# Output stage: the order of loads behind stores, one-hots made on two engines, and a shorter lag of the last step

## The chip, the core and the metric

The kernel runs on one core of a Trainium2 chip. A core has TensorE (PE), VectorE (DVE), ScalarE (ACT), GpSimd (POOL) and SyncE (SP, which here only issues DMAs). Each works through its own instruction stream in order, and they wait for each other by semaphores. The metric is the device time of the program in microseconds (us).

## What is computed

A layer of an xLSTM kind of attention with a decay (the first stage), then a layer in which a router lets each of 16 experts pick 2 of the 32 positions along the first axis, for each of the 512 places of the second, attend among the picked, and add their outputs back, followed by a residual and a layer norm. The part that matters here is the end:

```python
ao = jnp.einsum('hbid,hde->hbie', av, Wo) + bo
outs = jnp.zeros_like(t).at[b_ids, tok].add(ao)
y = t + outs
yn = (y - mu) * jax.lax.rsqrt(var + 1e-05) * ln_g + ln_b
# and, outside the layer: x = x + yn, x of shape (32, 512, 512), float32
```

Adding the experts' rows back to their tokens is a matrix product with a one-hot matrix: `hot[i, j] = (tokid[j] == colv[i])`.

## The kernel before

The program has three stages on one core: `recurrence_stage` (the largest part of the span), `expert_stage`, and `output_stage`, from 1398 us on. Only the last is touched. It works in **tiles** T = 0 to 127 of 128 rows by 512 elements; four tiles are a **half** H = 0 to 31 (1 MB), which is what SP loads and stores, in four DMAs each way. Five buffers `xt` (`x1_half0` to `x1_half3` and a part of `v_all`) hold the halves in turn.

The order of work is written out by hand, per engine:

- **SP** loads the first five halves (`load`, L1304). Then, for each half H, it waits until the half's four tiles are finished, stores it (L1311), and calls `load(H + 5)`, which waits until that same buffer's store has landed, since both use buffer H % 5.
- **PE**, in iteration T: `scatter(T)`, the one-hot product into one of two `z_ps` banks (L1464; it needs the one-hot, the rows of tile T, and the bank that VectorE's add of tile T - 2 has read); `rows(T + 2)`, four transposes into the single bank `r_ps` (L1456); in every second iteration `project` (L1445), as long as there is something to project; and in iterations 0, 4, 8, 12 of every 32, up to tile 76, `sums_by_head` (L1427), also through `r_ps`.
- **ACT**, in iteration T: `put_rows(T + 2)` evacuates `r_ps` (L1395, "the evacuation"); `square(T - 1)` makes the sum of squares (L1403); in every second iteration two `put_projection` (L1386); with head sums `put_sums` (L1376).
- **DVE**, in iteration T: `scale(T - 7)` (L1526), `add(T)` (L1520, the residual plus the scattered rows), `finish(T - 7)` (L1534), and, when T % 4 is 3, `mark(T // 4 + 2)` (L1510), which makes the four one-hot tiles of a half in one instruction of 128x512. Two halves' one-hots are kept. The 7 is `BEHIND`.
- **POOL**, for each tile: the addition of the final bias to x1 (L1344). After the addition of tile 4H + 1 it makes `ve` and `rs` (L1348, L1352), the scale factors of half H - 1, for which it needs that half's squares, and `finish` needs its `rs`. After tile 4H + 2, for the halves H = 0, 5 to 8 and 13 to 16, `attend` (L1330, L1332, L1336) multiplies attention weights and values for the head sums of a later group (twice for H = 0).

Of the setup, two lines matter: `XR, ZR, LEAD, BEHIND = 5, 8, 18, 7`, and `hot`, two tensors of 128x4x128. The end of the stage is the tail after `add(127)`, in which VectorE scales and finishes the last tiles, and the last stores.

## Time and profile before

| | us |
|---|---|
| three runs: lowest, median, highest | 1745.84, 1745.97, 1746.75 |
| profiled execution, its own time | 1738.19 |
| its span, first to last instruction | 1736.4 |
| VectorE busy over the span | 1398.5 (81%) |
| PE, POOL, ACT busy over the span | 1554.1, 1262.1, 1154.4 |
| output stage in the span | 1398 to 1736.4 |

The shares over the whole span mix three stages with different limits, so they say little about this one. The rows further down are all of the profiled execution, with times counted from the start of its span. In a timeline row the first number is the start, the second the duration; instructions of one engine may overlap, so the time that one costs is read from start to start. A bracket at the end names how long the engine had been idle before and what released it.

### The profile page before, as it was taken

What the parts mean: (1) busy time and instruction counts of PE and PEld (TensorE: products, weight loads), DVE (VectorE), ACT (ScalarE), POOL (GpSimd) and SP (SyncE); (2) the same over time, 40 slices, a digit from 0 to 9 for tenths busy, and PEclk for the clock granted to TensorE, in tenths of its full rate; (3) what the DMA queues carried; (4) which work ended last, traced back from release to release, by engine and by line L of the source; (5) the groups of instructions that cost most, each with busy time, mean ns of one, the idle gap of its engine ahead of it and who ended that gap; (6) DMA issues with size and microseconds to landing.
All of it is one profiled execution on the core that took longest, in us unless ns stands there. A gap on an engine that the chain in (4) does not pass through costs nothing. (4 is left out here: it accounts for less than half of the span.)

```text
span 1736.4 us, 58211 instructions
## 1 busy us (share of the span) xinstructions
PE 1554.1 (90%) x21967; PEld 1257.7 (72%) x22095; DVE 1398.5 (81%) x2826; ACT 1154.4 (66%) x2775; POOL 1262.1 (73%) x1235
## 2 busy tenths in 40 slices
PE   4899999999999999999999999679999969998983
PEld 3777777777777777777777777579999945555541
DVE  2588888888888888888888888768766458999998
ACT  3677777777777777777777776422334338888873
POOL 1477787777778777777877877757887527979764
PEclk9899999999999999999999999889999989999998
DMA  6133322233222333222323211173565354777787
GB/s 219 46 99 100 99 94 93 93 103 102 94 93 93 99 100 100 94 93 93 103 97 98 93 51 39 45 294 112 169 205 147 98 121 112 213 231 218 224 228 208
DMA packets 82020, 217.72 MB, mean 125 GB/s; under 512 B 13136, under 2 KB 14544, under 8 KB 72784
## 3 DMA queue, kind: packets, MB, share of 16 engines
q1 hardware_dynamic: 71504, 180.42, 33.4%
q0 software_dynamic: 10240, 33.56, 6.7%
q8 instruction: 180, 2.95, 0.7%
...
## 5 line engine op out<-in xcount | busy, mean ns | idle before, releaser
L315 POOL TENSOR_TENSOR rec_hn<-rec_hn,rec_out_w 128x512 f32<-128x512 f32 x128 | 183.3, 1432 | 124.5 <-DVE rec_hn L747 124.5
L293 POOL TENSOR_TENSOR rec_hrs<-rec_harg,rec_minus_half 128x8 f32<-128x8 f32 x128 | 253.9, 1983 | 10.0
L767 DVE TENSOR_TENSOR rec_x_ring<-rec_x_ring,rec_hn 128x512 f32<-128x512 f32 x128 | 88.7, 693 | 121.8 <-POOL rec_hn L315 121.4
L543 ACT ACTIVATE rec_d<-rec_l_ps 128x512 f32<-128x512 f32 x256 | 151.4, 592 | 52.2 <-PE rec_l_ps L447 50.8
L713 DVE TENSOR_TENSOR rec_c<-rec_s_ps,rec_d 128x512 f32<-128x512 f32 x256 | 166.4, 686 | 13.8 <-ACT rec_d L543 4.9
L1013 PE MATMUL exp_q_ps<-exp_wqkv,exp_rows_t 128*128 128x192 f32 x1024 | 177.1, 327 | 0.0
L1344 POOL TENSOR_TENSOR out_x_half<-out_x_half,ln_b 128x512 f32<-128x512 f32 x104 | 132.7, 1282 | 54.3 <-DVE out_z L1520 53.5
L964 POOL DMA_INDIRECT exp_x_rows<-x_scratch,rowid x128 | 135.0, 1055 | 45.8 <-issue 24.2
L467 PE MATMUL rec_o_ps<-rec_v_one,rec_c 128*64 128x65 f32 x4096 | 151.9, 226 | 16.8 <-DVE rec_c L713 16.8
L1013 PEld LDWEIGHTS exp_q_ps<-exp_wqkv,exp_rows_t 128*128 128x128 f32 x1024 | 165.4, 191 | 0.1
L1073 ACT ACTIVATE exp_rows_t<-exp_t_ps 128x512 f32<-128x512 f32 x128 | 69.4, 594 | 139.5 <-PE exp_t_ps L1001 139.5
L278 POOL TENSOR_TENSOR rec_v_one<-rec_ctx_ring,rec_gates 128x512 f32<-128x512 f32 x128 | 161.6, 1262 | 0.0
L1464 PE MATMUL out_z_ps<-probs_all,out_hot 128*128 128x512 f32 x256 | 138.4, 622 | 21.2 <-DVE out_z L1520 19.6
L467 PEld LDWEIGHTS rec_o_ps<-rec_v_one,rec_c 128*64 128x64 f32 x4096 | 132.4, 138 | 33.3 <-DVE rec_c L713 21.0
L423 PE MATMUL rec_s_ps<-rec_q_t,rec_k_t 64*128 64x128 f32 x2048 | 150.0, 286 | 0.0
L423 PEld LDWEIGHTS rec_s_ps<-rec_q_t,rec_k_t 64*128 64x128 f32 x2048 | 125.4, 189 | 21.4 <-issue 20.8
L1456 PEld LDWEIGHTS out_r_ps<-ident,out_ao_t 128*128 128x128 f32 x512 | 59.9, 141 | 93.7 <-issue 50.5
L525 ACT ACTIVATE rec_q_t<-rec_tp_ps 128x512 f32<-128x512 f32 x128 | 76.4, 597 | 72.0 <-PE rec_tp_ps L356 71.5
L567 ACT ACTIVATE rec_num<-rec_o_ps 128x260 f32<-128x260 f32 x256 | 84.8, 384 | 59.1 <-PE rec_o_ps L467 56.6
L447 PEld LDWEIGHTS rec_l_ps<-rec_rows,rec_sel_m 128*128 128x128 bf16 x1024 | 78.5, 98 | 60.9 <-issue 0.5
L1395 ACT ACTIVATE probs_all<-out_r_ps,sigma_rows 128x512 f32<-128x512 f32 x128 | 87.9, 687 | 50.7 <-PE out_r_ps L1456 49.2
L720 DVE TENSOR_TENSOR rec_q_inter<-rec_q_t,rec_em 128x512 f32<-128x512 f32 x96 | 115.8, 1206 | 1.7 <-ACT rec_em L543 1.2
...
## 6 DMA issues: line engine op xcount, KB each, us to landing
rec_x_ring<-in_x SPq DMA_DIRECT2D x128, 256.0 KB, 2.9
rec_ctx_ring<-in_ctx SPq DMA_DIRECT2D x128, 256.0 KB, 3.0
x_scratch<-rec_x_ring SPq DMA_DIRECT2D x128, 256.0 KB, 2.0
out_x_half<-x_scratch SPq DMA_DIRECT2D x104, 256.0 KB, 5.0
out<-out_x_half SPq DMA_DIRECT2D x104, 256.0 KB, 5.6
...
```

Source lines behind the costliest of these rows:

```text
L278: nc.gpsimd.tensor_tensor(v1[:, G % VR, :, 0:DH], cin[:, G % CR, :].rearrange("p (h d) -> p h d", h=NH), mean, ALU.subtract).then_inc(v1_d ...
L293: nc.gpsimd.tensor_tensor(hrs[:, G % 2], harg[:, G % 2], mhalf[:], ALU.pow).then_inc(hrs_done, 1)
L315: nc.gpsimd.tensor_tensor(h, h, w8[:], ALU.mult).then_inc(hw_done, 1)
L423: mm = nc.tensor.matmul(s_ps[e][:, k * P:(k + 1) * P], kt[r, t, k, :], qt[r, t, k, :], start=True, stop=True)
L467: mm = nc.tensor.matmul(o_ps[e][s:s + DH, k * V:(k + 1) * V], cmat[e][:, k, s:s + DH], v1[:, g % VR, 2 * k + e, :], start=(c == 0), stop=( ...
L543: nc.scalar.activation(dst[:].rearrange("p k s -> p (k s)"), l_ps[:], ACT.Exp).then_inc(l_read, 1)
L713: vec.tensor_tensor(cmat[e][:].rearrange("p k s -> p (k s)"), s_ps[e][:], dmat[e][:].rearrange("p k s -> p (k s)"), ALU.mult).then_inc(c_d ...
L720: vec.tensor_tensor(qe[G % 2][:], qt[:, G % TR], em[G % 2][:], ALU.mult).then_inc(qe_done, 1)
L964: nc.gpsimd.indirect_dma_start(xg[m % RING][:, i, :], None, x1_rows, bass.IndirectOffsetOnAxis(ap=rowid[:, c, h, i:i + 1], axis=0)).then_i ...
L1013: mm = nc.tensor.matmul(q_ps[m % 2][:, i * W3:(i + 1) * W3], gt[m % 2][:, i, k, :], w[:, h, k, :], start=(k == 0), stop=(k == KC - 1))
L1344: nc.gpsimd.tensor_tensor(x1, x1, lb[:], ALU.add).then_inc(xb_done, 1)
L1464: nc.tensor.matmul(z_ps[T % 2][:], hot[T // 4 % 2][:, T % 4, :], ao[T % 4], start=True, stop=True).then_inc(z_full, 1)
```

## The change

It does three things, all in the output stage:

- **SP.** After storing half H (from H = 1 on) it calls `load(H + 4)` in place of `load(H + 5)`. That load goes into the buffer of half H - 1, whose store was issued one half earlier.
- **One-hots.** VectorE makes them for even halves only, in iterations with T % 8 = 4, one half ahead. Those of odd halves are made by ACT, tile by tile and with two activations of 128x128: `dist = |tokid - colv|`, then `relu(1 - dist)`, which is 1 at equal integers and 0 else. One of the two stands at the end of every ACT iteration, the first in odd iterations and the second in even ones. There is one set of one-hots for even and one for odd halves; PE waits for the set that it needs.
- **Lag.** `BEHIND` is 6, and POOL makes `rs` after the addition of tile 4H in place of 4H + 1.

```diff
@@ -1247,7 +1247,7 @@
     PIECES = 2 * KC * z.S // POS
     TILES = z.S // 4
     HALVES = TILES // 4
-    XR, ZR, LEAD, BEHIND = 5, 8, 18, 7
+    XR, ZR, LEAD, BEHIND = 5, 8, 18, 6
 
     def sb(name, shape, dt=F32):
         return scope.enter_context(nc.sbuf_tensor("out_" + name, shape, dt))
@@ -1264,7 +1264,9 @@
     avt = [sb(f"av_t{p}", [P, HP, 2, P]) for p in range(2)]
     aot = [sb(f"ao_t{p}", [P, KC, POS, 2 * NE]) for p in range(2)]
     ao = [spare[:, p].rearrange("p h b -> p (h b)") for p in range(4)]
-    hot = [sb(f"hot{p}", [P, 4, P]) for p in range(2)]
+    dist = sb("distance", [P, P])
+    even_hot = sb("even_hot", [P, 4, P])
+    odd_hot = sb("odd_hot", [P, 4, P])
     xt = [sb(f"x1_half{r}", [P, 4, E]) for r in range(XR - 1)] + [
         vall[:, 0].rearrange("p h i d -> p (h i d)").rearrange("p (q e) -> p q e", e=E)]
     zt = [sb(f"z{r}", [P, E]) for r in range(ZR)]
@@ -1282,7 +1284,7 @@
     t0_done, t1_done, av_done = sem("t0_done"), sem("t1_done"), sem("av_done")
     at_full, at_read = sem("at_full"), sem("at_read")
     p_full, p_read, r_full, r_read = sem("p_full"), sem("p_read"), sem("r_full"), sem("r_read")
-    hot_done, z_full, z_read = sem("hot_done"), sem("z_full"), sem("z_read")
+    dist_done, even_done, odd_done, z_full, z_read = sem("dist_done"), sem("even_done"), sem("odd_done"), sem("z_full"), sem("z_read")
     ve_done, rs_done, square_done = sem("ve_done"), sem("rs_done"), sem("square_done")
     zg_done, xb_done, out_done = sem("zg_done"), sem("xb_done"), sem("out_done")
     x_in = [sem(f"x_in{r}") for r in range(XR)]
@@ -1309,8 +1311,8 @@
             sp.wait_ge(out_done, 4 * (H + 1))
             for j in range(4):
                 sp.dma_start(o_view[H, j], xt[H % XR][j * NB:(j + 1) * NB]).then_inc(o_st[H % XR], 16)
-            if H + XR < HALVES:
-                load(H + XR)
+            if H >= 1 and H + XR - 1 < HALVES:
+                load(H + XR - 1)
         for r in range(XR):
             sp.wait_ge(o_st[r], 64 * ((HALVES - 1 - r) // XR + 1))
 
@@ -1337,13 +1339,13 @@
 
         for n in range(2):
             attend(1, n)
-        for T in range(TILES + 3):
+        for T in range(TILES + 1):
             if T < TILES:
                 pool.wait_ge(z_read, T + 1)
                 x1 = xt[T // 4 % XR][:, T % 4, :]
                 nc.gpsimd.tensor_tensor(x1, x1, lb[:], ALU.add).then_inc(xb_done, 1)
             H, q = divmod(T, 4)
-            if q == 1 and H:
+            if q == 0 and H:
                 pool.wait_ge(square_done, 4 * H)
                 nc.gpsimd.tensor_tensor(ve[H % 2][:], var[H % 3][:], epsv[:, 4 * H - 4:4 * H], ALU.add).then_inc(ve_done, 1)
                 pool.wait_ge(ve_done, H)
@@ -1394,6 +1396,17 @@
                 act.wait_ge(z_full, T - 3)
             nc.scalar.activation(ao[T % 4], r_ps[:], ACT.Copy, scale=sgs[:, T:T + 1]).then_inc(r_read, 1)
 
+        def mark(T, part):
+            H, q = divmod(T, 4)
+            i = 4 * (H // 2) + q
+            if part == 0:
+                after(act, odd_done, i)
+                nc.scalar.activation(dist[:], tokid[:], ACT.Abs, bias=colv[:, T:T + 1], scale=-1.0).then_inc(dist_done, 1)
+            else:
+                act.wait_ge(dist_done, i + 1)
+                after(act, z_full, T - 7)
+                nc.scalar.activation(odd_hot[:, q, :], dist[:], ACT.Relu, bias=1.0, scale=-1.0).then_inc(odd_done, 1)
+
         def square(T):
             H, q = divmod(T, 4)
             act.wait_ge(z_read, T + 1)
@@ -1414,6 +1427,10 @@
                 put_projection((T + LEAD) // 2)
             if T >= 0 and T % 32 in (0, 4, 8, 12) and T // 32 + 1 < NC:
                 put_sums(4 * (T // 32 + 1) + T % 32 // 4)
+            q, part = divmod((T + 3) % 8, 2)
+            U = T + 7 - (T + 3) % 8 + q
+            if 4 <= U < TILES:
+                mark(U, part)
 
     @block.tensor
     def _(pe):
@@ -1459,9 +1476,14 @@
 
         def scatter(T):
             pe.wait_ge(r_read, T + 1)
-            pe.wait_ge(hot_done, T // 4 + 1)
+            H, q = divmod(T, 4)
+            if H % 2:
+                pe.wait_ge(odd_done, 4 * (H // 2) + q + 1)
+            else:
+                pe.wait_ge(even_done, H // 2 + 1)
+            hot = odd_hot if H % 2 else even_hot
             after(pe, z_read, T - 1)
-            nc.tensor.matmul(z_ps[T % 2][:], hot[T // 4 % 2][:, T % 4, :], ao[T % 4], start=True, stop=True).then_inc(z_full, 1)
+            nc.tensor.matmul(z_ps[T % 2][:], hot[:, q, :], ao[T % 4], start=True, stop=True).then_inc(z_full, 1)
 
         for n in range(4):
             sums_by_head(n)
@@ -1507,8 +1529,8 @@
             full = [P, 4, P]
             if H >= 2:
                 dve.wait_ge(z_full, 4 * (H - 1))
-            vec.tensor_tensor(hot[H % 2][:], tokid[:].unsqueeze(1).broadcast_to(full),
-                              colv[:, 4 * H:4 * H + 4].unsqueeze(2).broadcast_to(full), ALU.is_equal).then_inc(hot_done, 1)
+            vec.tensor_tensor(even_hot[:], tokid[:].unsqueeze(1).broadcast_to(full),
+                              colv[:, 4 * H:4 * H + 4].unsqueeze(2).broadcast_to(full), ALU.is_equal).then_inc(even_done, 1)
 
         def add(T):
             H, q = divmod(T, 4)
@@ -1538,7 +1560,6 @@
             attend(n)
         dve.wait_ge(gain_set, 1)
         mark(0)
-        mark(1)
         for u in range(1, 8, 2):
             put_projection(u)
         for T in range(TILES + BEHIND):
@@ -1548,8 +1569,8 @@
                 add(T)
             if T >= BEHIND:
                 finish(T - BEHIND)
-            if T % 4 == 3 and T // 4 + 2 < HALVES:
-                mark(T // 4 + 2)
+            if T % 8 == 4 and T // 4 + 1 < HALVES:
+                mark(T // 4 + 1)
 
 
 def program(nc, x, ctx, consts, gate_w, gate_b, out_w, wg, wqkv, bqkv, wo_in, vecs, out, x1_dram):
```

The order of instructions on the engines, as the built programs have it, at three places. First VectorE from iteration 11 into 13, before: L1526 is scale, L1520 add (`z3`, `z4` belong to tiles 11 and 12), L1534 finish, L1510 a mark.

```order
L1526 TENSOR_TENSOR out_zg_ps0<-out_z4,out_g_ps 128x512
L1520 SCALAR_TENSOR_TENSOR out_z3<-out_x1_half2,x1_means,out_z_ps1 128x512
L1534 SCALAR_TENSOR_TENSOR out_x1_half1<-out_zg_ps0,out_rs2,out_x1_half1 128x512
L1510 TENSOR_TENSOR out_hot0<-tokid,colv 128x512
L1526 TENSOR_TENSOR out_zg_ps1<-out_z5,out_g_ps 128x512
L1520 SCALAR_TENSOR_TENSOR out_z4<-out_x1_half3,x1_means,out_z_ps0 128x512
L1534 SCALAR_TENSOR_TENSOR out_x1_half1<-out_zg_ps1,out_rs2,out_x1_half1 128x512
L1526 TENSOR_TENSOR out_zg_ps0<-out_z6,out_g_ps 128x512
L1520 SCALAR_TENSOR_TENSOR out_z5<-out_x1_half3,x1_means,out_z_ps1 128x512
```

The same place in the change, where scale is L1548, add L1542, finish L1556 and the mark L1532:

```order
L1548 TENSOR_TENSOR out_zg_ps0<-out_z6,out_g_ps 128x512
L1542 SCALAR_TENSOR_TENSOR out_z4<-out_x1_half3,x1_means,out_z_ps0 128x512
L1556 SCALAR_TENSOR_TENSOR out_x1_half1<-out_zg_ps0,out_rs2,out_x1_half1 128x512
L1532 TENSOR_TENSOR out_even_hot<-tokid,colv 128x512
L1548 TENSOR_TENSOR out_zg_ps1<-out_z7,out_g_ps 128x512
L1542 SCALAR_TENSOR_TENSOR out_z5<-out_x1_half3,x1_means,out_z_ps1 128x512
L1556 SCALAR_TENSOR_TENSOR out_x1_half1<-out_zg_ps1,out_rs2,out_x1_half1 128x512
L1548 TENSOR_TENSOR out_zg_ps0<-out_z0,out_g_ps 128x512
L1542 SCALAR_TENSOR_TENSOR out_z6<-out_x1_half3,x1_means,out_z_ps0 128x512
```

The mark that stood behind tile 11 stands behind tile 12, the next one comes eight tiles on, and the tile scaled and finished is six back: beside the add of `z4` stands the scale of `z6` in place of `z5`.

Second ACT, iterations 9 to 11, before: L1395 is the evacuation `put_rows`, L1403 the square, L1386 the projection.

```order
L1395 ACTIVATE probs_all<-out_r_ps,sigma_rows 128x512
L1403 ACTIVATE out_squares,out_variance0<-out_z0 128x512
L1395 ACTIVATE probs_all<-out_r_ps,sigma_rows 128x512
L1403 ACTIVATE out_squares,out_variance0<-out_z1 128x512
L1386 ACTIVATE out_ao_t1<-out_p_ps0,bo_t 128x64x4x2
L1386 ACTIVATE out_ao_t1<-out_p_ps1,bo_t 128x64x4x2
L1395 ACTIVATE probs_all<-out_r_ps,sigma_rows 128x512
L1403 ACTIVATE out_squares,out_variance0<-out_z2 128x512
```

And in the change, with L1397, L1416 and L1388 for these, L1404 for the distance and L1408 for the Relu:

```order
L1397 ACTIVATE probs_all<-out_r_ps,sigma_rows 128x512
L1416 ACTIVATE out_squares,out_variance0<-out_z0 128x512
L1404 ACTIVATE out_distance<-tokid,colv 128x128
L1397 ACTIVATE probs_all<-out_r_ps,sigma_rows 128x512
L1416 ACTIVATE out_squares,out_variance0<-out_z1 128x512
L1388 ACTIVATE out_ao_t1<-out_p_ps0,bo_t 128x64x4x2
L1388 ACTIVATE out_ao_t1<-out_p_ps1,bo_t 128x64x4x2
L1408 ACTIVATE out_odd_hot<-out_distance 128x128
L1397 ACTIVATE probs_all<-out_r_ps,sigma_rows 128x512
L1416 ACTIVATE out_squares,out_variance0<-out_z2 128x512
```

The distance has come behind the square of an odd iteration, the Relu between the projection and the evacuation of the next.

Third SP, where the first loads into used buffers are issued, before (L1311 store, L1304 load):

```order
L1311 DMA out<-out_x1_half0 32x2048 x4
L1304 DMA out_x1_half0<-x1_scratch 32x2048 x4
L1311 DMA out<-out_x1_half1 32x2048 x4
L1304 DMA out_x1_half1<-x1_scratch 32x2048 x4
L1311 DMA out<-out_x1_half2 32x2048 x4
L1304 DMA out_x1_half2<-x1_scratch 32x2048 x4
```

In the change (L1313 store, L1306 load):

```order
L1313 DMA out<-out_x1_half0 32x2048 x4
L1313 DMA out<-out_x1_half1 32x2048 x4
L1306 DMA out_x1_half0<-x1_scratch 32x2048 x4
L1313 DMA out<-out_x1_half2 32x2048 x4
L1306 DMA out_x1_half1<-x1_scratch 32x2048 x4
L1313 DMA out<-out_x1_half3 32x2048 x4
```

A load now follows the store of the half after the one whose buffer it fills.

## Rows read from the trace of the kernel before

**Rows 1.** Engine busy by stretch: us, PE, PEld, DVE, ACT, POOL busy (instructions), clock, DMA

```profile
1640.30:1702.60 62.30, 52.20 (x309) 30.40 (x306) 62.30 (x93) 48.12 (x104) 43.68 (x43) 1.00 0.82 228
```

**Rows 2.** DVE timeline: start us, us, engine, line, operation, out<-in; iteration 84

```profile
1622.50 1.32 DVE L1510 TENSOR_TENSOR out_hot<-tokid,colv 128x512 f32<-128x512 f32 x1
1623.74 0.68 DVE L1526 TENSOR_TENSOR out_zg_ps<-out_z,out_g_ps 128x512 f32<-128x512 f32 x1
...
1625.66 0.68 DVE L1526 TENSOR_TENSOR out_zg_ps<-out_z,out_g_ps 128x512 f32<-128x512 f32 x1
```

**Rows 3.** PE timeline, transposes of iterations 12, 14 and 16

```profile
1454.25 0.63 PE L1456 MATMUL out_r_ps<-ident,out_ao_t 128*128 128x128 f32 x4
...
1459.66 0.63 PE L1456 MATMUL out_r_ps<-ident,out_ao_t 128*128 128x128 f32 x4
...
1463.85 0.63 PE L1456 MATMUL out_r_ps<-ident,out_ao_t 128*128 128x128 f32 x4
```

**Rows 4.** ACT timeline of the same stretch

```profile
1456.11 1.34 ACT L1386 ACTIVATE out_ao_t<-out_p_ps,bo_t 128x512 f32<-128x512 f32 x2
1457.32 0.60 ACT L1376 ACTIVATE out_av_t<-out_r_ps 128x512 f32<-128x512 f32 x1
...
1461.53 1.35 ACT L1386 ACTIVATE out_ao_t<-out_p_ps,bo_t 128x512 f32<-128x512 f32 x2
1462.91 0.69 ACT L1395 ACTIVATE probs_all<-out_r_ps,sigma_rows 128x512 f32<-128x512 f32 x1
1463.50 0.62 ACT L1403 ACTIVATE out_squares<-out_z 128x512 f32<-128x512 f32 x1
...
1464.52 0.69 ACT L1395 ACTIVATE probs_all<-out_r_ps,sigma_rows 128x512 f32<-128x512 f32 x1 [0.30 <-PE out_r_ps L1456]
```

**Rows 5.** ACT timeline of the first stage, its narrow activations

```profile
501.58 1.06 ACT L555 ACTIVATE rec_decayed<-rec_state,rec_em 128x65 f32<-128x65 f32 x4
...
516.65 0.26 ACT L602 ACTIVATE rec_rows_in<-rec_gm 128x64 bf16<-128x64 f32 x1
516.80 0.25 ACT L630 ACTIVATE rec_ex<-rec_ex_arg 128x64 f32<-128x64 f32 x1
```

**Rows 6.** Groups by line, ACT, whole span: count | busy us, mean ns | idle before

```profile
L519 ACT ACT_TABLE_LOAD x1 | 1.3, 1283 | 0.7 <-PEq L1641 0.7
```

**Rows 7.** POOL timeline at the head sums

```profile
1480.21 1.27 POOL L1344 TENSOR_TENSOR out_x_half<-out_x_half,ln_b 128x512 f32<-128x512 f32 x1
1481.45 1.06 POOL L1330 TENSOR_TENSOR out_av<-v_all,att 128x512 f32<-128x512 f32 x1
...
1491.55 1.51 POOL L1330 TENSOR_TENSOR out_av<-v_all,att 128x512 f32<-128x512 f32 x1
```

**Rows 8.** DVE timeline, the marker instructions of the walk through the stage

```profile
1466.08 0.73 DVE L1520 SCALAR_TENSOR_TENSOR out_z<-v_all,x_means,out_z_ps 128x512 f32<-128x512 f32 x1
...
1478.81 0.74 DVE L1520 SCALAR_TENSOR_TENSOR out_z<-out_x_half,x_means,out_z_ps 128x512 f32<-128x512 f32 x1
...
1520.69 0.75 DVE L1534 SCALAR_TENSOR_TENSOR out_x_half<-out_zg_ps,out_rs,out_x_half 128x512 f32<-128x512 f32 x1 [1.33 <-POOL out_rs L1352]
...
1540.77 0.73 DVE L1520 SCALAR_TENSOR_TENSOR out_z<-out_x_half,x_means,out_z_ps 128x512 f32<-128x512 f32 x1
...
1628.17 0.74 DVE L1520 SCALAR_TENSOR_TENSOR out_z<-out_x_half,x_means,out_z_ps 128x512 f32<-128x512 f32 x1
...
1718.15 0.75 DVE L1520 SCALAR_TENSOR_TENSOR out_z<-out_x_half,x_means,out_z_ps 128x512 f32<-128x512 f32 x1
...
1729.22 0.75 DVE L1534 SCALAR_TENSOR_TENSOR out_x_half<-out_zg_ps,out_rs,out_x_half 128x512 f32<-128x512 f32 x1
```

**Rows 9.** SP timeline, the load issues of two halves in a row

```profile
1630.40 1.70 SPq L1304 DMA_DIRECT2D out_x_half<-x_scratch  x4
...
1639.67 2.04 SPq L1304 DMA_DIRECT2D v_all<-x_scratch  x4
```

**Rows 10.** Source view of line 1304 in the stage, its landing times

```profile
DMA to landing us min/median/max: 3.2/5.0/16.8
```

## The prediction

> **What bounds the kernel now.** The change touches only the last stage, from 1398 us to the end of the span at 1736.4, so I read the windows of that stage first. In a late stretch VectorE is busy 62.30 of 62.30 us, PE 52.20, ACT 48.12, POOL 43.68, and the DMA share is 0.82 [rows 1]: VectorE sets the pace there, and the reader should see that ACT and PE are only some 15 to 25% below it. The VectorE timeline gives the price of an iteration: scale to scale is 1.92 us (1623.74 to 1625.66), and a one-hot instruction (mark) puts 1.24 us in front of one in four (1622.50 to 1623.74) [rows 2]. The stretch of [rows 1] runs from mark to mark over seven halves: 62.30 / 7 = 8.90 us a half, 2.225 a tile, and (8.90 - 1.24) / 4 = 1.915 for a tile without its mark, which I use.
>
> Next, what comes behind VectorE. Over tiles 10 to 18 VectorE was late and PE ran ahead of it, so its own loop is seen. The loop covers two tiles, because the projection comes every second tile: 1459.66 to 1463.85 is 4.19 us, and 1454.25 to 1459.66, a pair with a head sum in it, is 5.41 [rows 3]. It runs through the single r_ps bank: ACT empties it, PE transposes into it, ACT empties it. So PE and ACT together can do 2.095 us a tile, 9.60 us for a half with a head sum.
>
> Third, POOL. In the eight halves from tile 22 and from tile 54 it also multiplies attention sums (L1330 to L1336). The same instruction recurs after 10.10 us (1481.45 to 1491.55) [rows 7], and VectorE stands 1.33 us waiting for rs [rows 8]. There POOL is the bound.
>
> **The change part by part.** *One-hots.* VectorE loses every odd mark, 15 of them after tile 4, and keeps one per eight tiles: (8 x 1.915 + 1.24) / 8 = 2.07 us a tile. That is less than the PE/ACT loop's 2.095, so PE and ACT come last next, and the gain of 0.155 us a tile is cut to what they leave.
>
> ACT gets one narrow activation per tile, in every iteration: the distance in odd ones, behind the square, and the Relu in even ones, behind the projection. No 128x128 activation is in the trace, so I bound it (a gain is excluded, ACT only issues more). Below: a 128x64 activation is followed by the next after 0.15 us (516.65 to 516.80); four of 128x65 with a per-partition scale take 1.06 us, 0.26 each [rows 5]. Above: a 512-wide activation with a per-partition bias goes every 0.605 us (two from 1456.11 to 1457.32) [rows 4]. Both new ones are far nearer the narrow rows. From 0.15, and 64 elements at the slope between the 64 and 512 wide rows (about 0.83 ns each), I take 0.20 for the Relu, and 0.28 for the distance, whose bias is a per-partition operand. Each has a cover. The distance comes before an evacuation that now waits 0.30 us for PE (at 1464.52) [rows 4]: hidden. The Relu comes between a projection pair (1461.53 + 1.21 = 1462.74) and the evacuation at 1462.91 [rows 4]: 0.17 us of cover for 0.20 us, and what sticks out lengthens the PE/ACT loop directly, since that evacuation is in it. I add 0.07 for the pair, between 0.03 and the 0.15 that a Relu of its full duration would cost: 4.26 us, 2.13 a tile. In pairs with a head sum the Relu is covered by PE's wait for the bank. PE issues as much as before, with one more counter to look at.
>
> The Trainium skill, ScalarE: Activation LUTs, section What ACT_TABLE_LOAD costs, states that an ACTIVATE takes 186 ns + 0.833 ns per element, 93 ns more for each per-partition operand, and that neighbours overlap by 93 ns. By it the two would be 0.20 and 0.29, an estimate from that page. The narrow rows agree; no row has this shape.
>
> The same section prices every switch of function set at 2.66 us, which would speak against new functions on ACT. The trace has one table load in the whole span [rows 6], though Abs and Relu already run between Exp and Square in the first stage, so I price it at nothing.
>
> *Finish six back.* Iterations before the last add do the same work, but one scale and finish pair moves from the tail to where VectorE now has gaps. The tail's steps are (1729.22 - 1718.15 - 0.66) / 7 = 1.49 us [rows 8]: 1.5 us gained. The factor rs is made one tile earlier too, behind the bias addition of tile 4H+4 in place of 4H+5, so it still has two iterations. In the POOL-bound stretches the chain from POOL's addition of tile 22 to the rs that VectorE waits for has one addition less, 1.25 us, and rs no longer stands ahead of that addition: it started at 1480.21, 0.55 later than its add at 1478.81 (done 1479.55, plus 0.1) allowed [rows 7, 8]. Together 1.8 us per stretch.
>
> *SP.* The load now comes one store later, but waits for a buffer whose store was issued a half before. SP no longer stands between store and load. Before, the turn from load to load took 9.27 us (1630.40 to 1639.67) [rows 9], longer than VectorE's 8.9: loads slipped 0.37 us per half, hidden by the buffers in hand. At 8.5 us a half that slip would have become a stall; the edit itself is worth nothing beyond keeping it away. Queued behind the load on SP is only the next store. The eight transfers land within about 9.3 us of the store's start, by the same turn; the data is used seven iterations later, 7 x 2.07 - 1.4 = 13 us. So 4 us of cover.
>
> **The sum**, walked along the stage, by the VectorE markers [rows 8]:
> - To add of tile 16: before 1466.08. PE had its tile ready when it began the transposes behind it at 1463.85 [rows 3], 2.2 us earlier. After, VectorE has lost the marks at iterations 11 and 15 for one at 12, and PE is some 0.7 us later through the new ACT work: 1464.6, gain 1.5.
> - Tiles 16 to 22: before 12.73 (1478.81 - 1466.08); after 6 x 1.915 + 1.24 = 12.73 (a mark falls in at 20), or 12.78 by PE. Gain 0.
> - POOL-bound stretch, to finish of tile 32: 1.8. Then 1520.69 becomes 1517.4.
> - To add of tile 48: before 1540.77. After, one and a half iterations (3.2) and eight more with a mark (16.5): 1537.1; by PE two pairs with sums and two without, 19.3, about 1536.6. Gain 0.4. Tiles 48 to 54: 0.
> - The second POOL-bound stretch repeats both: 2.2.
> - Tiles 86 to 127: before 1718.15 - 1628.17 = 89.98. After, up to 110 by the PE/ACT loop, 24 x 2.13 = 51.1; from 110 no projection is left and VectorE leads, 17 x 1.915 + 1.24 = 33.8. Gain 5.1.
> - Tail: 1.5.
>
> Sum 12.5. The span would be 1723.9 us. The profiled execution took 1738.19 us for a span of 1736.4, and the median of the three runs is 1745.97, 7.8 above it; the gain carries over: 1745.97 - 12.5 = **1733.5 us**.
>
> **The rivals.** *A: ACT is dearer, or the three nearly full engines hold each other up.* ACT has 4.19 - 0.30 - 0.17 = 3.7 us of work in a pair; the marks make it 4.2 of 4.26. With the marks at their full durations, 0.31 and 0.40, a pair is 4.41: 0.075 more a tile, over some 42 tiles outside the POOL and head-sum stretches, 3.2 us. At 2.23 a tile, 4.2. VectorE's 2.07 is so near that a late one-hot or square is not made up either. 1736.5 to 1742.5, about 1739. For it: two engines above 95%. Against: both new activations lie in measured gaps.
>
> *B: VectorE alone sets the pace.* If the Relu hides fully, tiles 86 to 127 take 41 x 1.915 + 4 x 1.24 = 83.5 instead of 84.9: 1732.1. Against: 2.095 a tile is PE's measured best.
>
> *C: it gives nothing.* The marks at 0.5 us each bring ACT to 4.7 a pair, 2.35 a tile, 9 us lost on the 42 tiles and most of the rest in the halves with head sums: 1743 to 1749. Against: nothing narrow in the trace costs that.
>
> *D: the loads come too late, and it is slower.* A half's buffer is reloaded four halves on. From the first add of a half to the end of its last finish VectorE needs 9 x 1.915 + 1.24 + 1.4 = 19.9 us; the rest of four halves at the old pace, 35.6 - 19.9 = 15.7 us, is the point from which the landing, counted from the store, sets a pace slower than before. Before, one half more of buffer stood in hand. The turn gives 9.3, but one load's landing reached 16.8 [rows 10], and both directions now go at once at a share above 0.82. At 16.8 every four halves cost 1.1 more, over twenty halves 5.5, less the tail's 1.5: 1750.0.
>
> **How the numbers follow.** Forecast (1732 to 1736.5) 0.64, A 0.18, B 0.05, C 0.07, D 0.06. What a measurement of this kernel can tell from no change is about 0.2%, 3.5 us, so faster is 0.64 + 0.18 + 0.05 = 0.87, same 0.07 (C), slower 0.06 (D). The range leaves out C, D and a little of each end: 1731.0 to 1741.5.
>
> **What the profile after would show.** One-hots: 16 of them on VectorE; ACT's new lines at about 0.31 and 0.40 us duration, started 0.20 and 0.28 before their neighbours. Pace: adds of tiles 86 and 110 some 51 us apart; VectorE below 98% there with waits for out_z_ps, ACT above 95%; full again after 110. POOL stretches: the recurrence still 10.10. Tail: 9.6 us from the last add to the last finish. SP: no wait of a load for a store's landing. VectorE waits for x_scratch loads would prove D; a pair above 4.4 us with ACT never idle, A or C; a pair below 4.19, that PE's loop was read wrongly.

## The result, and the profile after

The changed kernel takes 1735.67 us (median, 1734.83 to 1736.45) against 1746.36 us for the kernel before in the same measurement: ratio 0.9937, 95% interval [0.9919, 0.9954]. A second measurement of both (b0, below) gives 0.9946 [0.9929, 0.9964]. It is faster, by some 0.5 to 0.6%; 1733.5 was forecast, with a range of 1731.0 to 1741.5.

The profiled executions stand differently to each other. That of the changed kernel took 1736.45 us (span 1734.6), that of the kernel before 1738.19 (span 1736.4). But VectorE's first head sum, the first work of the output stage, starts at 1398.66 us in the one and at 1404.76 in the other, although nothing ahead of it was changed. So I count the **stage**, from that instruction's start to the end of the span: 337.74 us before, 329.84 after, 7.9 us less.

The table cuts the stage at VectorE's adds (the number is the tile). Each entry is a difference of two start times of such add rows; "tail" runs from the start of add(127) to the end of the span. "Sum of the prediction" is the gain that its walk gave to the piece.

| piece | before | after | gain | sum of the prediction |
|---|---|---|---|---|
| start to add(16) | 67.42 | 67.01 | 0.4 | 1.5 |
| 16 to 22 | 12.73 | 13.51 | -0.8 | 0 |
| 22 to 48 | 61.96 | 60.43 | 1.5 | 2.2 |
| 48 to 54 | 12.74 | 13.86 | -1.1 | 0 |
| 54 to 80 | 61.93 | 60.44 | 1.5 | 2.2, with 80 to 86 |
| 80 to 86 | 12.73 | 13.50 | -0.8 | - |
| 86 to 127 | 89.98 | 84.41 | 5.6 | 5.1 |
| tail | 18.25 | 16.68 | 1.6 | 1.5 |
| stage | 337.74 | 329.84 | 7.9 | 12.5 |

The markers from VectorE's timeline of the changed kernel (start us, us, engine, line, operation, tiles), to be held against [rows 8]: adds of tiles 16, 22, 86, 110 and 127, and the last finish.

```profile
1471.77 0.74 DVE L1542 SCALAR_TENSOR_TENSOR out_z<-v_all,x_means,out_z_ps 128x512 f32<-128x512 f32 x1
...
1485.28 0.74 DVE L1542 SCALAR_TENSOR_TENSOR out_z<-out_x_half,x_means,out_z_ps 128x512 f32<-128x512 f32 x1
...
1633.51 0.74 DVE L1542 SCALAR_TENSOR_TENSOR out_z<-out_x_half,x_means,out_z_ps 128x512 f32<-128x512 f32 x1
...
1684.15 0.73 DVE L1542 SCALAR_TENSOR_TENSOR out_z<-out_x_half,x_means,out_z_ps 128x512 f32<-128x512 f32 x1
...
1717.92 0.76 DVE L1542 SCALAR_TENSOR_TENSOR out_z<-out_x_half,x_means,out_z_ps 128x512 f32<-128x512 f32 x1
...
1727.51 0.75 DVE L1556 SCALAR_TENSOR_TENSOR out_x_half<-out_zg_ps,out_rs,out_x_half 128x512 f32<-128x512 f32 x1
```

From 86 to 110 the pace is 50.64 / 24 = 2.11 us a tile, and PE's timeline gives the same number: one pair of tiles, from transposes to transposes, takes 1557.77 - 1553.55 = 4.22 us, where [rows 3] had 4.19.

```profile
1553.55 0.63 PE L1473 MATMUL out_r_ps<-ident,out_ao_t 128*128 128x128 f32 x4 [0.16 <-issue]
...
1557.77 0.63 PE L1473 MATMUL out_r_ps<-ident,out_ao_t 128*128 128x128 f32 x4 [0.15 <-issue]
```

ACT's timeline of the same stretch holds the two new operations, against [rows 4]:

```profile
1553.77 0.42 ACT L1404 ACTIVATE out_distance<-tokid,colv 128x128 f32<-128x128 f32 x1
1554.21 0.69 ACT L1397 ACTIVATE probs_all<-out_r_ps,sigma_rows 128x512 f32<-128x512 f32 x1
...
1556.63 0.32 ACT L1408 ACTIVATE out_odd_hot<-out_distance 128x128 f32<-128x128 f32 x1
1556.82 0.70 ACT L1397 ACTIVATE probs_all<-out_r_ps,sigma_rows 128x512 f32<-128x512 f32 x1
```

The evacuation follows the Relu after 0.19 us, forecast 0.20. It follows the distance after 0.44, but that is PE's time: the transposes that it reads end at 1553.55 + 0.63 = 1554.18, so the distance is hidden as forecast.

In the window view of this part of the stage (us, then busy time and instructions of PE, PEld, DVE, ACT, POOL, granted clock, DMA share, GB/s) three engines are all but full, where [rows 1] had VectorE alone:

```profile
1644.34:1678.02 33.68, 32.52 (x225) 19.67 (x224) 33.26 (x51) 33.55 (x81) 25.89 (x25) 1.00 0.95 250
```

### The profile page after: what moved, and what is told of

Its sections match the earlier page's. It is cut to its first block and busy times, and to the rows that moved or that the text cites. A ratio compares the mean times of both kernels' runs of the same rounds, so it can differ in the third digit from the quotient of the medians.

```text
span 1734.6 us, 58383 instructions
## 1 busy us (share of the span) xinstructions
PE 1557.3 (90%) x21967; PEld 1258.2 (73%) x22095; DVE 1382.2 (80%) x2810; ACT 1180.2 (68%) x2903; POOL 1263.1 (73%) x1235
## 5 line engine op out<-in xcount | busy, mean ns | idle before, releaser
L267 POOL TENSOR_TENSOR rec_k_weighted<-rec_ctx_ring,rec_ex 128x512 f32<-128x512 f32 x96 | 114.5, 1192 | 0.0
L445 PE MATMUL rec_l_ps<-rec_sel_g,rec_rows 128*128 128x512 bf16 x256 | 96.9, 379 | 19.1 <-issue 16.4
```

What stands on the lines that cost most here:

```text
L267: nc.gpsimd.tensor_tensor(kw[:, outer(G) % 2], cin[:, G % CR, :].rearrange("p (h d) -> p h d", h=NH), w, ALU.mult).then_inc(kw_done, 1)
```

## The experiments

The pieces of the stage, for all kernels that follow, read as in the table above:

| kernel | to 16 | 16-22 | 22-48 | 48-54 | 54-80 | 80-86 | 86-110 | 110-127 | tail | stage |
|---|---|---|---|---|---|---|---|---|---|---|
| before | 67.42 | 12.73 | 61.96 | 12.74 | 61.93 | 12.73 | 53.40 | 36.58 | 18.25 | 337.74 |
| a4 before again | 67.40 | 12.73 | 61.96 | 12.72 | 61.94 | 12.73 | 53.39 | 37.26 | 18.22 | 338.35 |
| a1 SP alone | 68.30 | 12.73 | 61.96 | 12.72 | 61.90 | 12.73 | 53.41 | 36.42 | 18.14 | 338.31 |
| a3 lag alone | 68.63 | 12.73 | 62.74 | 12.73 | 62.78 | 12.72 | 53.41 | 36.65 | 16.76 | 339.15 |
| a2 one-hots alone | 66.13 | 13.53 | 58.83 | 13.53 | 58.86 | 13.51 | 52.40 | 38.89 | 18.13 | 333.81 |
| a5 the same | 66.15 | 13.51 | 58.91 | 13.56 | 58.90 | 13.56 | 57.56 | 39.60 | 18.19 | 339.94 |
| b1 SP and one-hots | 66.14 | 13.51 | 58.85 | 13.67 | 58.76 | 13.84 | 53.35 | 35.94 | 18.13 | 332.19 |
| changed | 67.01 | 13.51 | 60.43 | 13.86 | 60.44 | 13.50 | 50.64 | 33.77 | 16.68 | 329.84 |
| b0 changed again | 67.03 | 13.51 | 60.45 | 13.87 | 60.44 | 13.51 | 50.67 | 33.80 | 16.67 | 329.95 |
| b2 no ACT marks | 66.97 | 13.45 | 60.43 | 13.80 | 60.40 | 13.45 | 50.24 | 33.79 | 16.74 | 329.27 |
| b3 late first finish | 66.13 | 13.51 | 60.42 | 13.89 | 60.48 | 13.53 | 50.66 | 33.79 | 16.66 | 329.07 |
| c1 spread sums | 67.02 | 13.52 | 58.08 | 14.60 | 57.74 | 14.24 | 50.62 | 33.79 | 16.63 | 326.24 |
| c2 spread and late | 66.16 | 13.52 | 58.11 | 14.60 | 57.73 | 14.28 | 50.64 | 33.78 | 16.71 | 325.53 |
| c3 and tail marks | 66.16 | 13.53 | 58.21 | 14.58 | 57.83 | 14.27 | 50.36 | 32.54 | 16.73 | 324.21 |

**The control and the edits one by one.** a4 is the kernel before, unchanged.

> The kernel before, unchanged, to see how far the stages ahead of the output stage differ between executions. In the profiled executions so far VectorE's first head sum starts at 1398.66 us in the kernel before and at 1404.76 in the changed one, though nothing ahead of it was changed. My theory: that is the execution, not the change: here the start lies anywhere from 1398 to 1406, the output stage is 337.7 us within 0.5, and the time is that of the kernel before. Rival: the start is always near 1398.7 in the kernel before, and the change costs 6 us ahead of the stage.

1.0001 [0.9990, 1.0012]. (Here and below these are the ratio to the kernel before beside it and its 95% interval.) The first head sum starts at 1403.85 us here and at 1398.66 in the first profile: the start belongs to the execution, not to the change. The stage is 338.35, 0.6 more than in the first profile, all of it between 110 and 127, where an add waits 0.9 us for x1 data.

a1 changes the order on SP alone:

```diff
-            if H + XR < HALVES:
-                load(H + XR)
+            if H >= 1 and H + XR - 1 < HALVES:
+                load(H + XR - 1)
```

> The kernel before with only the order on SP changed: the next x1 half is loaded behind the following store. The one-hots, BEHIND and the place of the rsqrt stay. My theory: the loads were never late in the kernel before (in its trace no add waits for x1 data), so the output stage, from VectorE's first head sum to the end of the span, stays at 337.7 us within 1, and the time at the before's within 2. Rival: the SP queue held back the stores or the loads already, and this edit alone carries a part of the 10.7 us: a stage of 335 us or less.

0.9999 [0.9987, 1.0011]; stage 338.31. As forecast, nothing. (Its first piece is 0.9 us longer; where that comes from stands in the last section.)

a3 changes the lag alone, and with it the place of rs on POOL:

```diff
-    XR, ZR, LEAD, BEHIND = 5, 8, 18, 7
+    XR, ZR, LEAD, BEHIND = 5, 8, 18, 6
-        for T in range(TILES + 3):
+        for T in range(TILES + 1):
-            if q == 1 and H:
+            if q == 0 and H:
```

> The kernel before with only BEHIND 6 in place of 7 and the rsqrt one tile earlier on POOL. My theory: the loop's last adds come no earlier (VectorE has the same work), the tail behind the last add is shorter by 1.5 us, POOL's chain in its three stretches of attends is shorter by up to 1.8 us each, and the start loses about 1 us as finish(0) waits for its rsqrt: a stage of 334 to 336.5 us. Rival: only the tail, 336.2 less what the start loses, 337; or nothing at all, since a finish that comes a tile earlier only moves its work ahead of the adds.

1.0009 [0.9999, 1.0020]; stage 339.15, 0.8 longer than the control: outside what my theory allowed, and 2 us past its first rival. The time moves by less than its noise, so the second rival, nothing at all, comes nearest. The tail is 1.5 shorter, as said. The start loses 1.2 (expected: about 1). But each of the two POOL stretches is 0.8 *longer* (62.74 and 62.78 against 61.96 and 61.94), where my prediction had them 1.8 shorter.

**The one-hots alone.** a2 is the changed kernel with the three edits above taken back, so that only the sharing of the one-hots is left.

> The changed kernel's one-hots alone (odd halves in two narrow ACT operations a tile, even halves by one DVE mark in eight tiles), with SP's old order, BEHIND 7 and the rsqrt at the second tile of a half, as before. My theory: VectorE gains half of its marks (16 marks of 1.24 us less, 9 of them where it is the last) but once it is quicker the old SP turn of 9.27 us a half (store, then the load that waits for that store's landing) may end last somewhere behind tile 86: a stage near 335 us, with waits of add for the x1 data in the trace. Rival: the five buffers give the loads slack enough, no add waits for x1 data, and the stage is about 332 us, the tail's 1.5 and POOL's chain missing from the changed kernel's 329.8. A third: ACT's marks give all of it back, 337 or more.

Timed, it is *slower* than the kernel before: 1744.73 us, ratio 1.0025 [1.0013, 1.0036], though its profiled execution took 1735.36. The waits of VectorE and of SP's queue in that profile (engine, tile, line, waited for: us in total, times, longest):

```profile
DVE out_z L1542 <- DMA out_x_half<-x_scratch: 5.0, 4, 1.9
DVE out_z L1542 <- DMA v_all<-x_scratch: 1.5, 1, 1.5
```

```profile
SPq L1306 <- DMA out<-out_x_half: 91.5, 22, 5.2
SPq L1313 <- DVE out_x_half L1556: 52.9, 9, 43.9
SPq L1306 <- DMA out<-v_all: 20.4, 5, 4.7
```

SP stands 111.9 us at its loads (L1306) until a store has landed, and adds wait 6.5 us for x1 data. In the kernel before SP stands there as long, 114.7 us, but the adds wait only 0.2. Since a2's timed executions were some 9 us longer than this one, I ran the same kernel once more.

> The shared one-hots alone once more (SP's old order, BEHIND 7), for another profile: the first profiled execution took 1735.4 us, the ten timed ones 1741.4 to 1747.7. My theory: in the longer executions the stores and loads land later, SP's turn (store, wait for its landing, load) is longer than 9.27 us a half, and the waits of add for x1 data are 10 us or more in place of 6.5. Rival: these waits are 6.5 again and the stages ahead of the output stage are what differs.

This execution took 1745.81 us (1.0004 of the median of the kernel before beside it, without an interval). a5 ran on another chip than a2, where the kernel before takes 1745.13 us and not 1740.64. It is as long as a2's timed executions, and the same view shows a part of why:

```profile
DVE out_z L1542 <- DMA out_x_half<-x_scratch: 10.1, 7, 2.3
DVE out_z L1542 <- DMA v_all<-x_scratch: 2.5, 2, 1.8
```

12.6 us of waits in place of 6.5, and a stage of 339.94 in place of 333.81: the 6.1 us are the same. Its span is 10.5 us longer; the other 4.4 lie ahead of the stage (first head sum at 1404.06 in place of 1399.69). SP's timeline has the loads of eight halves from a first to a last:

```profile
1626.64 1.70 SPq L1306 DMA_DIRECT2D out_x_half<-x_scratch  x4
...
1693.82 1.70 SPq L1306 DMA_DIRECT2D v_all<-x_scratch  x4
```

67.18 / 7 = 9.60 us a half. These are halves 22 to 29; the same seven turns take 66.18 / 7 = 9.45 in a2 (1618.03 to 1684.21). The prediction read 9.27 a half from [rows 9]. Once VectorE needs only 8.4 us a half, the turn of SP, store, landing, load, is the bound, and the one-hots' gain turns into waits, in a5 all of it: from add(86) to add(110) that kernel takes 57.56 us, 9.59 a half, SP's own pace.

**One-hots and SP's order together**, and the changed kernel once more beside them. b1 is the changed kernel with the lag edit alone taken back.

> The changed kernel with BEHIND 7 and the rsqrt at the second tile of a half, as before: SP's new order and the shared one-hots together. The one-hots alone came out slower in the timed runs (1.0025) and had a turn of 9.27 us a half on SP from tile 104 on, with 6.5 us of waits of add for x1 data. My theory: SP's edit takes that away whole, no add waits for x1 data, and the stage is 331.5 to 333: the changed kernel's 329.8, plus 1.5 of the tail, plus POOL's chain, less 0.9 at the first pair with a head sum. So 0.9958 to 0.997. Rival: something else in the shared one-hots made them slow (ACT), and this kernel stays above 0.999.

> The changed kernel, unchanged, against the kernel before on one chip. My theory: its output stage is 329.8 us within 0.5 as in its first profile, the kernel before's is 338 as in three profiles so far (337.7, 338.3, 338.4), so the times differ by 8.0 to 8.5 us and the ratio is 0.9950 to 0.9955; the 10.7 us of the first comparison had some 2.5 us in it that came from stages that are the same in both. Rival: the change gains 10.7 again (0.9937 to 0.994).

b0: 0.9946 [0.9929, 0.9964], between what I expected and its rival; stage 329.95, within 0.1 of the first profile. (Of the three stages of "the kernel before" that I named, one was a1's.) b1: 0.9967 [0.9954, 0.9980], stage 332.19. Time and stage fit my expectation, its reason doesn't. In b1's view of waits adds still wait for x1 data:

```profile
DVE out_z L1542 <- DMA out_x_half<-x_scratch: 4.6, 5, 1.7
...
DVE out_z L1542 <- DMA v_all<-x_scratch: 0.9, 1, 0.9
```

These are not waits for a turn of SP. They come at every second half, and what is short is the time between a load's issue and its first use. From b1's timelines, SP's load of half 25 and the add(100) that uses it:

```profile
1649.54 3.22 SPq L1306 DMA_DIRECT2D out_x_half<-x_scratch  x4
```

```profile
1657.73 0.75 DVE L1542 SCALAR_TENSOR_TENSOR out_z<-out_x_half,x_means,out_z_ps 128x512 f32<-128x512 f32 x1 [0.80 <-DMA out_x_half<-x_scratch]
```

Issue 3.22 and the median landing of 5.1 make 8.3 us, and VectorE is there after 8.2 - 0.8 = 7.4. In the changed kernel the finish that lets a store go, and with it the load behind it, comes one iteration earlier. There the same load is issued at 1652.68, behind the store at 1649.92, and add(100) starts at 1662.21 without a wait: 9.5 us. SP's and VectorE's timeline of the changed kernel:

```profile
1649.92 2.71 SPq L1313 DMA_DIRECT2D out<-out_x_half  x4
1652.68 3.24 SPq L1306 DMA_DIRECT2D out_x_half<-x_scratch  x4
```

```profile
1662.21 0.74 DVE L1542 SCALAR_TENSOR_TENSOR out_z<-out_x_half,x_means,out_z_ps 128x512 f32<-128x512 f32 x1
```

Its landings in the stage, from the source view of line 1306, and then SP's waits from the view of waits, none of them at L1306:

```profile
DMA to landing us min/median/max: 4.4/5.3/6.6
```

```profile
SPq L1313 <- DVE out_x_half L1556: 120.6, 26, 42.6
SPq L1313 <- DVE v_all L1556: 17.6, 6, 4.8
SPq L1317 <- DMA out<-out_x_half: 3.1, 1, 3.1
```

So no edit makes the kernel faster alone (0.9999, 1.0009 and 1.0025); the one-hots with SP's order give 0.9967, and all three 0.9946. The one-hots bring the gain, SP's order removes the turn, the lag gives the loads their lead. The one-hots with the lag, but without SP's order, were not run. And b1 shows what the lag costs. Against it the changed kernel loses 0.9 us to add(16), and 1.6 and 1.7 in the two POOL stretches; it wins 2.7 from 86 to 110, 2.2 from 110 to 127 and 1.5 in the tail.

The waits for rs tell the same. From the views of waits over the stage, first the line of the kernel before, then of b1, then of the changed kernel:

```profile
DVE out_x_half L1534 <- POOL out_rs L1352: 9.3, 8, 2.0
```

```profile
DVE out_x_half L1556 <- POOL out_rs L1354: 10.0, 8, 2.0
```

```profile
DVE out_x_half L1556 <- POOL out_rs L1354: 14.8, 8, 3.6
```

**What ACT's marks cost.** b2 builds ACT's one-hots once, for half 1, and uses them for every odd half, so that 120 of ACT's narrow operations are left out and the later odd halves are scattered by the wrong rows:

```diff
-            if 4 <= U < TILES:
+            if 4 <= U < 8:
                 mark(U, part)
...
-                pe.wait_ge(odd_done, 4 * (H // 2) + q + 1)
+                pe.wait_ge(odd_done, min(q + 1 if H == 1 else 4, 4))
```

> The changed kernel with ACT's one-hots built for half 1 alone and used for every odd half (the scatters of the later odd halves put their rows by the wrong one-hots; 120 narrow ACT operations are left out). It prices what ACT's marks cost the changed kernel. My theory: next to nothing, a pair of tiles goes from 4.22 to 4.19 us and only where PE and ACT are the limit: a stage of 329 to 329.8. Rival: three nearly full engines hold each other up, and ACT's marks are why 6 tiles behind each stretch of head sums cost 13.5 to 13.9 us in place of 12.7: then the stage is 326.5 or less.

0.9946 [0.9924, 0.9967], the changed kernel's ratio; stage 329.27, 0.6 to 0.7 shorter. In PE's timeline of b2 the pair is back at 4.19:

```profile
1550.70 0.63 PE L1473 MATMUL out_r_ps<-ident,out_ao_t 128*128 128x128 f32 x4
...
1554.89 0.63 PE L1473 MATMUL out_r_ps<-ident,out_ao_t 128*128 128x128 f32 x4
```

The six tiles behind each stretch still cost 13.45 and 13.80. So the marks on ACT cost 0.6 us of a stage, and of the 0.8 to 1.1 lost at each transition only 0.06 is theirs.

**The first finish.** In the changed kernel finish(0) waits longest, ahead of add(7). VectorE's line, and PE's transposes before and behind the head sum at tile 8:

```profile
1451.08 0.75 DVE L1556 SCALAR_TENSOR_TENSOR out_x_half<-out_zg_ps,out_rs,out_x_half 128x512 f32<-128x512 f32 x1 [3.63 <-POOL out_rs L1354]
```

```profile
1450.99 0.63 PE L1473 MATMUL out_r_ps<-ident,out_ao_t 128*128 128x128 f32 x4
...
1455.69 0.63 PE L1473 MATMUL out_r_ps<-ident,out_ao_t 128*128 128x128 f32 x4 [1.36 <-ACT out_av_t L1378]
...
1457.29 0.63 PE L1473 MATMUL out_r_ps<-ident,out_ao_t 128*128 128x128 f32 x4
```

The pair takes 6.30 us. b3 finishes tiles 0 and 1 behind add(7):

```diff
-            if T >= BEHIND:
-                scale(T - BEHIND)
+            lagging = [] if T <= BEHIND else [0, 1] if T == BEHIND + 1 else [T - BEHIND]
+            for t in lagging:
+                scale(t)
             if T < TILES:
                 add(T)
-            if T >= BEHIND:
-                finish(T - BEHIND)
+            for t in lagging:
+                finish(t)
```

> The changed kernel, but VectorE finishes nothing in its iteration 6, and tiles 0 and 1 behind add(7) in iteration 7. In the changed kernel finish(0) stands ahead of add(7) and waits 3.63 us for its rsqrt; ACT's square of tile 7 and its copy of the head sum behind it come late, and the pair at tile 8 takes 6.30 us on PE in place of 5.42. My theory: that pair comes back to 5.42 and add(16) comes 0.8 to 0.9 us earlier than in the changed kernel (66.1 from the stage's start in place of 67.0), and the end is 0.5 to 0.9 us earlier. Rival: add(16) gains, but the stretch of POOL that follows takes it back, and the end is where it was.

0.9940 [0.9923, 0.9958]; stage 329.07. add(16) comes at 66.13 in place of 67.03, and everything behind it keeps its length, so 0.8 to 0.9 us reach the end. In PE's timeline of b3 the pair is 5.43:

```profile
1448.68 0.63 PE L1473 MATMUL out_r_ps<-ident,out_ao_t 128*128 128x128 f32 x4 [0.16 <-issue]
...
1452.50 0.63 PE L1473 MATMUL out_r_ps<-ident,out_ao_t 128*128 128x128 f32 x4 [0.65 <-ACT out_av_t L1378]
...
1454.11 0.63 PE L1473 MATMUL out_r_ps<-ident,out_ao_t 128*128 128x128 f32 x4
```

**The head sums spread out.** c1 puts the head sums of chunks 2 and 3 every eight tiles, and POOL's attends ten tiles ahead of each:

```diff
+    sum_at = {32 * c - 32 + 4 * n if c == 1 else 32 * c - 40 + 8 * n: 4 * c + n for c in range(1, NC) for n in range(4)}
+    sum_of = {k: T for T, k in sum_at.items()}
+    attend_at = {sum_of[k] - 10: k for k in range(8, 4 * NC)}
...
+            if T == 2:
+                attend(1, 2)
+                attend(1, 3)
+            if T in attend_at:
+                attend(*divmod(attend_at[T], 4))
...
-            if T >= 0 and T % 32 in (0, 4, 8, 12) and T // 32 + 1 < NC:
-                sums_by_head(4 * (T // 32 + 1) + T % 32 // 4)
+            if T in sum_at:
+                sums_by_head(sum_at[T])
```

> The changed kernel with the head sums of chunks 2 and 3, and POOL's attends for them, every 8 tiles in place of every 4 (sums at tiles 24, 32, ... 80, attends 10 tiles ahead). In the changed kernel POOL is the limit between tiles 22 and 48 and between 54 and 80 (10.1 us a half), and behind each such stretch six tiles cost 13.5 to 13.9 us in place of 12.7. My theory: from add(22) to add(86) the pace is then that of PE and ACT alone, 16 x 2 pairs at 4.22 plus 8 head sums at 1.2 = 144.6 us in place of 148.2, so a stage of 326.2 within 0.7. Rival: it is not the place of the sums; what POOL no longer limits, the delivery of PE does (a sum pair in every fourth pair), and the gain is under 1.5 us.

> The spread head sums and the late first finish (tiles 0 and 1 finished behind add(7)) together, on the changed kernel. My theory: the gains add up, since the one lies ahead of add(16) and the other behind add(22): a stage of 325.5 (329.9 less 0.8 less 3.6), ratio to the kernel before 0.992. Rival: the first stretch takes the 0.8 back, 326.2.

c1: 0.9924 [0.9910, 0.9939], stage 326.24. From add(22) to add(86) it takes 144.66 us in place of 148.23; 144.6 was forecast. c2, with the late first finish: 0.9917 [0.9903, 0.9930], stage 325.53. The gains add up. In c2 VectorE's waits for rs over the stage are down from 14.8 to 3.1 us, and it waits for PE instead (view of waits):

```profile
DVE out_z L1544 <- PE out_z_ps L1488: 22.5, 29, 3.4
...
DVE out_x_half L1558 <- POOL out_rs L1357: 3.1, 7, 0.7
```

**Two more marks to ACT.** c3 adds to c2 a tile-wise one-hot on ACT for halves 28 and 30, in iterations 105 to 119; PE's scatters of these halves wait for them:

```diff
+        def tail_mark(T):
+            H, q = divmod(T, 4)
+            i = 4 * ((H - 28) // 2) + q
+            after(act, tail_done, i)
+            act.wait_ge(z_full, T - 7)
+            nc.scalar.activation(tail_dist[:], tokid[:], ACT.Abs, bias=colv[:, T:T + 1], scale=-1.0).then_inc(tail_dist_done, 1)
+            act.wait_ge(tail_dist_done, i + 1)
+            nc.scalar.activation(even_hot[:, q, :], tail_dist[:], ACT.Relu, bias=1.0, scale=-1.0).then_inc(tail_done, 1)
...
+            if T % 2 and 105 <= T < 121:
+                tail_mark(8 * ((T + 7) // 8) + (T + 7) % 8 // 2)
...
-            if T % 8 == 4 and T // 4 + 1 < HALVES:
+            if T % 8 == 4 and T // 4 + 1 < 28:
```

> The kernel with spread head sums and late first finish, and the one-hots of the last two even halves (28 and 30) made by ACT too, in narrow operations tile by tile: VectorE has two marks of 1.24 us less behind tile 104, where the projections run out and ACT has room. My theory: behind tile 110 VectorE is the limit, so its last marks come off the end: 1.2 to 2.5 us less than without this edit, a stage of 323 to 324.3. Rival: ACT's 16 more narrow operations (0.42 and 0.20 us) delay its copies while projections still run (to tile 108), and the gain is under 0.6.

1727.99 us, 0.9908 [0.9895, 0.9921]; stage 324.21. From 110 to 127 it takes 32.54 in place of 33.78: one mark's worth, the smaller end of what I expected. The other mark that VectorE lost stood at tile 108, ahead of add(110), where PE and ACT set the pace, and gives 0.3 (50.36 against 50.64). c3 beats both kernels, the changed one by 5.6 to 5.7 us of stage. From c2 its interval does not part it; the stage does, by 1.3 us.

Not tried is the combination that the table suggests: a finish seven back up to tile 80, where the lag of six costs 0.9, 1.6 and 1.7, and six back from there on, where the loads need it.

## Why the prediction was right, and where its steps were not

**The loop that comes last next: right.** VectorE at 2.07 a tile is quicker than PE and ACT's loop, and that loop was sized at 2.13 with ACT's new work; it measures 2.11 (4.22 a pair). The 51.1 us for tiles 86 to 110 came out as 50.64, the 33.8 from 110 on as 33.77. The prices of ACT's operations, taken from the narrow rows [rows 5], stood: 0.19 for the Relu against 0.20, the distance hidden. (The slope of "about 0.83 ns" an element is not quite what the rows give: between the rows of 65 and 512 with a per-partition operand it is (0.605 - 0.26) / 447, 0.77 ns. On 64 elements that is less than 0.01 us.) ACT's timeline of c3 shows both once more, the distance followed by an operation that waits for nobody, and the Relu by an evacuation:

```profile
1681.99 0.39 ACT L1408 ACTIVATE out_distance<-tokid,colv 128x128 f32<-128x128 f32 x1
1682.29 0.39 ACT L1419 ACTIVATE out_tail_distance<-tokid,colv 128x128 f32<-128x128 f32 x1
1682.71 0.31 ACT L1421 ACTIVATE out_even_hot<-out_tail_distance 128x128 f32<-128x128 f32 x1
1682.93 0.67 ACT L1401 ACTIVATE probs_all<-out_r_ps,sigma_rows 128x512 f32<-128x512 f32 x1
```

The distance's own step is 0.30 us, the Relu's 0.22 here and 0.19 in the loop. The formula of the Trainium skill (ScalarE: Activation LUTs, What ACT_TABLE_LOAD costs) had given 0.29 and 0.20 as estimates: the trace agrees.

What sticks out of the Relu is 0.03 a pair, not 0.07; b2 puts the whole at 0.6 us of a stage. The term for 86 to 127, 5.1, measured 5.6; the tail's 1.5 measured 1.5 in a3. Rival C is out, and so is A's high price for ACT, although its condition (two engines above 95%) came true. B is out too: even without ACT's marks (b2) the pace is 50.24 / 24 = 2.09 us, PE's, and not VectorE's 2.07. The prediction looked for VectorE below 98% in this stretch; it is at 33.26 / 33.68, 98.8%.

**"Finish six back", in the POOL-bound stretches: the step failed, and its size was right only by luck.** The prediction gave each stretch 1.8 us because the chain from POOL's addition to rs is one addition shorter. a3, which has this edit alone, is 0.8 us *slower* in each stretch. With the one-hots in place, the edit costs 1.6 and 1.7 (b1 against the changed kernel). What the step forgot is that finish comes a tile earlier too, ahead of one add more: the wait for rs then stands in front of work that PE and ACT are waiting for. Between add(22) and add(48) a3 has no more waits for rs than the kernel before (4.1 us against 4.4, summed over the timeline's brackets). But ACT waits 1.2 us for adds (none before), PE 4.1 for ACT's copies of the head sums (2.6), and POOL 0.4 for PE's head sum (none). Against b1, the changed kernel shows the same: 1.2 against none, 4.1 against 2.6, 0.7 against none, and here the waits for rs grow as well, 6.6 against 4.4. In a3's timeline add(32) to add(40) takes 21.50 us (20.21 before), although add(22) to add(32) is 0.5 shorter; that 0.5 is what is seen of the 1.8. All these runs move rs and the finish together, so what each does alone is not shown.

The gain of 1.5 in these stretches comes from the marks instead: the one-hots alone take 3.1 off each (58.83 and 58.86 against 61.96 and 61.93), of which the lag gives 1.6 back; the prediction counted it as nothing, since it held POOL to be the bound at 10.10 us a half. POOL is the bound there: from its first to its last attend of a stretch its rows wait for no other engine. But the 10.10 [rows 7] is not all its own work. VectorE's mark and POOL's instructions hold each other up. In the kernel before VectorE's mark starts at 1491.05, and the attend product (one of the two multiplications that begin an attend) that starts beside it, at 1491.55 [rows 7], takes 1.51 us; in a2 no mark is under way there, and the same product takes 1.06. The mark of the kernel before, then POOL's row of a2:

```profile
1491.05 1.09 DVE L1510 TENSOR_TENSOR out_hot<-tokid,colv 128x512 f32<-128x512 f32 x1
```

```profile
1491.64 1.06 POOL L1332 TENSOR_TENSOR out_av<-v_all,att 128x512 f32<-128x512 f32 x1
```

Behind 1420 us the kernel before has twenty attend products (L1330 and L1332 there): the eight that start during a mark take 1.50 to 1.51 us, the other twelve 1.05 to 1.06. In a2 (L1332 and L1334) none starts during a mark, and all take 1.06 or 1.07. So 0.45 us of each 10.10 came from VectorE, and the recurrence falls to 9.66 (1491.64 - 1481.98 in a2), or 9.93 where a mark meets POOL's third operation. Of the 3.1 us, 1.1 lie between the first and the last attend and 2.1 behind the last, where VectorE leads again and has fewer marks. The sign "still 10.10" did not come true either: in the changed kernel the recurrences are 9.66, 10.46 and 10.07, with POOL's new waits for PE in the longer ones.

**The transitions: the step failed.** For tiles 16 to 22 the prediction took the larger of two totals, 12.73 by VectorE or 12.78 by PE. It is 13.51, at all three places 0.8 to 1.1 too long, and in every kernel that shares the one-hots. VectorE's timeline of the changed kernel shows the mechanism, with adds of tiles 17 and 19 and then the mark:

```profile
1474.07 0.75 DVE L1542 SCALAR_TENSOR_TENSOR out_z<-v_all,x_means,out_z_ps 128x512 f32<-128x512 f32 x1 [0.29 <-PE out_z_ps L1486]
...
1478.28 0.75 DVE L1542 SCALAR_TENSOR_TENSOR out_z<-v_all,x_means,out_z_ps 128x512 f32<-128x512 f32 x1 [0.29 <-PE out_z_ps L1486]
...
1481.52 1.33 DVE L1532 TENSOR_TENSOR out_even_hot<-tokid,colv 128x512 f32<-128x512 f32 x1
```

Up to tile 20 VectorE has caught up with PE and waits for it: 1480.20 - 1471.77 = 8.43 us for four tiles, two pairs of 4.22. Then the mark falls in, and the next two tiles go by VectorE: 5.08 us. The two engines are within 2% of each other here (2.07 and 2.11 us a tile) and VectorE's work is lumpy, so the totals don't decide; the waits before the lump are lost. From 86 on the mark falls in every eight tiles too, but there VectorE works off what piled up behind one mark until the next one comes: eight tiles take 16.88 us, PE's four pairs, against 16.56 of its own work (8 x 1.915 + 1.24), and the totals do decide.

**The start: a term mis-sized.** To add(16) the gain was put at 1.5 and is 0.4. finish(0) in iteration 6 waits 3.63 us, and ACT's square of tile 7 and its copy of the head sum come late; that is 0.8 to 0.9 (b3). The prediction named the wait for rs only in the later stretches.

**SP: right, and with less cover than told.** No load waits for a store's landing. That 9.27 us a half would have become a stall is what a2 and a5 show: without SP's edit (and the lag's) the one-hots alone are slower than the kernel before. "4 us of cover" was too much. Half 25 in the changed kernel has 12.3 us from the start of the store ahead of its load (1649.92) to add(100) (1662.21), where 13 were forecast, but the transfers need 2.8 + 3.2 + 5.3 = 11.3, not the 9.3 of the old turn. That leaves 1.0; with the lag of before it is less than none (b1). Rival D's mechanism was nearer than its chance of 0.06 said: one iteration of lag keeps it away, though b1, with 5.5 us of such waits, is still faster than the kernel before. The landing of 16.8 [rows 10] that D was built on belongs to the loads ahead of the first store, issued from 1398.6 to 1408.4; behind 1420 us the kernel before's longest is 6.3.

**The sum.** The walk gave 12.5 us, the stages differ by 7.9 (8.2 with the mean of both profiles of before), and the medians by 10.7 and 9.4. That the forecast of 1733.5 came within 2.2 us of 1735.67 owes something to this last difference. Where the 1 to 3 us between stage and median lie stays open. b0's interval runs from 6.3 to 12.4 us and holds the 8 of the stages, so a part or all of it may be noise. Both profiles of before show one add waiting for x1 data, 0.2 and 0.9 us, so its loads have no slack left either by the last halves, and longer executions might hold more such waits, as a5 does against a2. The one longer execution of it that was profiled speaks against that: a4's took 1743.96 us, 5.8 more than the first, and 5.2 of them lie ahead of the stage.
